# A three-layer decoder block on one core: chunk 0's second own terms and chunk 1's first state products moved ahead of the key units

## The reference, cut to what matters

```python
kh = jnp.einsum('bchd,bhde->bche', ki, S)
...
qh = jnp.einsum('bchd,bhde->bche', qi, S) - jnp.einsum('bhcs,bshe->bche', A, v_new)
o = qi + _ln(qh, w, b)
S = S - jnp.einsum('bchd,bche->bhde', ki * ei[..., None], v_new)
```

## Time and profile before

| | us |
|---|---|
| median of 3 runs | 380.12 |
| lowest and highest | 378.19 and 382.46 |
| the profiled execution, its time | 379.22 |
| its span in the trace | 377.5 |
| TensorE busy | 337.9 (89%) |
| VectorE busy | 264.6 (70%) |
| ScalarE busy | 202.0 (53%) |
| GpSimd busy | 75.7 (20%) |

### The profile page before, as it was taken

The page is one execution under the profiler, slowest core; times in us unless marked ns, Lnnn a source line. Parts: engine busy times, 40 slices in busy tenths (PEclk is TensorE's granted clock), DMA queues, the critical chain, the costliest instruction groups (busy, mean ns, idle before and its releaser), DMA issues.

```text
span 377.5 us, 11630 instructions
## 1 busy us (share of the span) xinstructions
PE 337.9 (89%) x5083; PEld 240.2 (64%) x5083; DVE 264.6 (70%) x537; ACT 202.0 (53%) x372; POOL 75.7 (20%) x91
## 2 busy tenths in 40 slices
PE   1999997996978785998999999999999999999974
PEld 1544585564534422687697796887977969866732
DVE  0499988897799899647263764855857739567795
ACT  1245974864545474346426555555565566576351
POOL 3009300000000000000062441522714405300100
PEclk9999999999999899799999999999999999999998
DMA  8997000000501203270040200200202000000000
GB/s 199 278 285 255 4 4 3 3 5 3 170 3 39 92 2 114 49 128 3 0 108 10 55 2 16 58 0 16 57 4 66 3 15 2 2 16 1 16 1 28
DMA packets 17987, 19.97 MB, mean 53 GB/s; under 512 B 3712, under 2 KB 15376, under 8 KB 17680
## 3 DMA queue, kind: packets, MB, share of 16 engines
q1 hardware_dynamic: 17328, 18.69, 18.3%
q10 hardware_dynamic: 608, 0.54, 0.7%
HBM read 18.04 MB, written 1.18 MB: 51 GB/s over the span
## 4 chain that ended last, share of the span: by engine, by line
PE 75%; DVE 13%; ACT 5%; issue 4%; DMA 1%; SPq 0%; POOLq 0%; POOL 0%; DVEq 0%; ACTq 0%
PE ps L795 14%; PE ps L729 14%; PE ps L550 6%; PE ps L772 5%; PE ps L787 5%; PE ps L665 4%; PE ps L503 3%; PE ps L814 3%; PE ps L841 2%; PE ps L745 2%; PE ps L531 2%; PE ps L521 2%; PE ps L620 2%; PE ps L763 2%; PE ps L655 2%
## 5 line engine op out<-in xcount | busy, mean ns | idle before, releaser
L729 PEld LDWEIGHTS ps<-x1t,xwq 128*128 128x128 f32 x512 | 59.2, 192 | 6.0 <-issue 4.2
L729 PE MATMUL ps<-x1t,xwq 128*128 128x128 f32 x512 | 62.1, 278 | 0.5 <-ACT x1t L1196 0.5
L795 PE MATMUL ps<-mvo,cxp 128*128 128x256 f32 x224 | 51.8, 383 | 0.5 <-ACT cxp L1207 0.5
L1909 POOL TENSOR_SCALAR rstd<-mv 128x1 f32<-128x1 f32 x20 | 4.4, 220 | 209.8 <-DVE mv L1650 209.8
L795 PEld LDWEIGHTS ps<-mvo,cxp 128*128 128x128 f32 x224 | 41.3, 190 | 6.6 <-ACT cxp L1207 0.8
L665 PE MATMUL ps<-ctxt,xwk 128*128 128x512 f32 x64 | 35.0, 656 | 3.9 <-ACT kt L1079 2.7
L1159 ACT ACTIVATE qt<-ps 128x512 f32<-128x512 f32 x32 | 19.1, 597 | 32.3 <-PE ps L729 32.3
L1077 ACT ACTIVATE ksq<-ps 128x512 f32<-128x512 f32 x32 | 19.0, 592 | 20.2 <-PE ps L665 13.3
L1079 ACT ACTIVATE kt<-ps,gks 128x512 f32<-128x512 f32 x32 | 21.9, 686 | 0.0
L1166 ACT ACTIVATE qsq<-ps 128x512 f32<-128x512 f32 x32 | 19.0, 593 | 4.7 <-PE ps L745 4.6
L772 PEld LDWEIGHTS ps<-kt,qt 128*64 128x64 f32 x512 | 16.2, 138 | 6.8 <-ACT qt L1159 3.8
(11 more groups left out here) (238 smaller groups left out, 681.3 us busy)
## 6 DMA issues: line engine op xcount, KB each, us to landing
rkb<-kscale SPq DMA_DIRECT2D x16, 256.0 KB, 4.1
ctx<-in_ctx_dram SPq DMA_DIRECT2D x4, 512.0 KB, 7.5
xwo<-in_L_xattn_Wo_dram SPq DMA_DIRECT2D x1, 2048.0 KB, 14.2
xwq<-in_L_xattn_Wq_dram SPq DMA_DIRECT2D x4, 512.0 KB, 4.4
w1n<-in_L_ffn_w_gate_up_dram SPq DMA_DIRECT2D x1, 1408.0 KB, 9.7
xwv<-in_L_xattn_Wv_dram SPq DMA_DIRECT2D x1, 1024.0 KB, 11.3
xwk<-in_L_xattn_Wk_dram SPq DMA_DIRECT2D x1, 1024.0 KB, 16.4
xn<-in_x_dram SPq DMA_DIRECT2D x2, 512.0 KB, 6.0
```

The source lines that it names most:

```text
L729: last = mm(bank(n % 2, P, t * P), xwq[qn][:, k * BANK + t * P:k * BANK + (t + 1) * P], x1t[:, (i % 2) * D + k * P:(i % 2) * D + (k + 1) * ...
L795: last = mm(bank(turn_banks[turn_of[("y", i, 0)]], D), context_of(i)[:, h * P:(h + 1) * P], mvo[:, h * D:(h + 1) * D], start=h == 0, stop= ...
```

## The change

PE: `own_terms(0,1)` and `state_products(1,0)` now stand directly behind the two `w2t` jobs, ahead of the wait for all jobs and of every key unit. `scores_ttt(1,1)` moves from behind `mvo` 7 to behind the first two key units. Ahead of `state_products(1,1)` there are 3 key units where there were 5; chunk 3 gets 13 where it had 11 (`KEY_PLACES`). `w2t` 0 takes bank 6, not 7.

ACT: the Sqrt with which the table is loaded moves from behind the first key unit to behind the copy of `s2`. All first three key units stand behind `state_root(1,0)` and the first output square; no key unit stands ahead of these.

DVE: `output_terms` is split. `query_terms(0)` and `query_terms(1)` (four products each) stand ahead of `after_own_terms(0,0)` and of `after_own_terms(0,1)`; the transpose stands behind `kb_rows(1)`. `a_masked(1)` moves behind `chain(1,0)`, `gate_terms` behind `after_own_terms(1,0)`.

```diff
--- before.py
+++ after.py
@@ -53,7 +53,7 @@
 GW = 2 * C + 32
 NKU = 2 * XH
 LT = NT - 1
-KEY_PLACES = [(1, 2), (2, 2, 1, 1, 2, 1), (2, 2, 1, 1, 2, 1), (2, 3, 3, 3)]
+KEY_PLACES = [(2, 1), (3, 2, 1, 1, 2, 1), (2, 2, 1, 1, 2, 1), (3, 3, 4, 3)]
 
 
 
@@ -313,7 +313,7 @@
             job("w2t", n, by="act")
         index_of = {(k, key): n for n, (k, key, _) in enumerate(jobs)}
         job_banks = [n % 8 for n in range(index_of[("s1", (0,))])]
-        job_banks += [(5, 6, 7, 0, 1, 2, 3)[n % 7] for n in range(len(jobs) - 1 - len(job_banks))] + [5]
+        job_banks += [(5, 6, 7, 0, 1, 2, 3)[n % 7] for n in range(len(jobs) - 2 - len(job_banks))] + [6, 5]
 
         def bank_left(n):
             return max(m for m in range(n) if job_banks[m] == job_banks[n])
@@ -621,7 +621,6 @@
                 done(last)
                 if n == 3:
                     scores_ttt(1, 0)
-            scores_ttt(1, 1)
             wait(emptied_by(index_of[("s1", (2,))]))
             pe.wait_ge(sem("diag_ready"), 2)
             bk = open_job("s2", 0)
@@ -639,6 +638,9 @@
                         last = nc.tensor.transpose(o[0:w, (t * KT + r) * P:(t * KT + r + 1) * P],
                                                    w2q[:, r * FF + k * P:r * FF + k * P + w], ident_b[:, :])
                 done(last)
+            wait(emptied_by(index_of[("s2", (0,))]))
+            own_terms(0, 1)
+            state_products(1, 0)
 
 
             def warm(bk, n):
@@ -678,12 +680,13 @@
                     key_unit(next(units))
 
             keys(KEY_PLACES[0][0])
-            own_terms(0, 1)
+            scores_ttt(1, 1)
             keys(KEY_PLACES[0][1])
             for c in range(1, NCH):
-                places = iter(KEY_PLACES[c])
-                state_products(c, 0)
-                keys(next(places))
+                places = iter(KEY_PLACES[c][1:])
+                if c > 1:
+                    state_products(c, 0)
+                    keys(KEY_PLACES[c][0])
                 state_products(c, 1)
                 keys(next(places))
                 if c < NCH - 1:
@@ -1056,6 +1059,7 @@
                 emptied(A(mvo[:, n * BANK:(n + 1) * BANK], bank(bk), ACT.Copy))
             bk = job_at("s2", 0)
             emptied(A(s2[:, :], bank(bk, D), ACT.Copy))
+            A(eps_t[:, 2:3], eps_t[:, 1:2], ACT.Sqrt)
             bk = job_at("w2t", 0)
             emptied(A(w2t[:, 0:3 * D], bank(bk).bitcast(BF16)[:, 0:3 * D], ACT.Copy))
             bk = job_at("w2t", 1)
@@ -1114,9 +1118,6 @@
                 for _ in range(n):
                     key_unit(next(units))
 
-            keys(KEY_PLACES[0][0])
-            A(eps_t[:, 2:3], eps_t[:, 1:2], ACT.Sqrt)
-            keys(KEY_PLACES[0][1])
             for c in range(1, NCH):
                 places = KEY_PLACES[c]
                 state_root(c, 0)
@@ -1506,12 +1507,13 @@
                 for h in range(2):
                     u_blocks(0, h)
 
+            def query_terms(hh):
+                dve.wait_ge(sem("prep_act"), emptied_by(index_of[("gate", (1, 1))])[1])
+                for c in range(NCH):
+                    V.scalar_tensor_tensor(out=chunk_half(sgR, c, hh), in0=kq_half(1, c, hh), scalar=wb[:, KT + hh:KT + hh + 1],
+                                           in1=chunk_half(tmp1, c, hh), op0=ALU.add, op1=ALU.mult).then_inc(sem("q_terms"), 1)
+
             def output_terms():
-                dve.wait_ge(sem("prep_act"), emptied_by(index_of[("gate", (1, 1))])[1])
-                for hh in range(KT):
-                    for c in range(NCH):
-                        V.scalar_tensor_tensor(out=chunk_half(sgR, c, hh), in0=kq_half(1, c, hh), scalar=wb[:, KT + hh:KT + hh + 1],
-                                               in1=chunk_half(tmp1, c, hh), op0=ALU.add, op1=ALU.mult).then_inc(sem("q_terms"), 1)
                 dve.wait_ge(sem("q_terms"), KT * NCH)
                 V.transpose(qbR[:, :], sgR[:, :]).then_inc(sem("out_terms"), 1)
 
@@ -1567,14 +1569,13 @@
             first_chains()
             for c in range(1, NCH):
                 p_rows(c)
+            query_terms(0)
+            after_own_terms(0, 0)
+            query_terms(1)
+            after_own_terms(0, 1)
+            kb_rows(1)
             output_terms()
-            after_own_terms(0, 0)
-            gate_terms()
-            after_own_terms(0, 1)
             for c in range(1, NCH):
-                if c == 1:
-                    kb_rows(c)
-                    a_masked(c)
                 if c == NCH - 1:
                     key_scales(0)
                 state_read(c, 0)
@@ -1584,12 +1585,16 @@
                     output_inverse(2 * c - 2)
                     out_c(c - 2)
                 chain(c, 0)
+                if c == 1:
+                    a_masked(c)
                 state_read(c, 1)
                 output_sums(2 * c - 1)
                 output_inverse(2 * c - 1)
                 chain(c, 1)
                 out_normed()
                 after_own_terms(c, 0)
+                if c == 1:
+                    gate_terms()
                 out_gated(c - 1)
                 after_own_terms(c, 1)
                 if c < NCH - 1:
```

## The result

The changed kernel's median is 380.33 us (12 runs), that of the kernel before 379.75 us (12 runs); the ratio of the recorded comparison is 1.006 with a 95% interval of 1.0031 to 1.0089. That is less than the 1% of the prediction's bound, so it counts as no change. The forecast was 380.7 and +1.0 us; the middle of the interval is +2.3 us. In a second comparison (experiment 5) the same kernel stood at 1.0012 (0.9982 to 1.0041), +0.5 us. The medians themselves lie 0.6 us apart in both comparisons (380.33 and 379.75, 379.60 and 378.95). So the two ratios put the loss at 0.6 and 0.1%, and whether there is one at all isn't settled. The ratios leave out executions that took over 1.5% more than the fastest of their kernel. The profiled execution took 381.24 us with a span of 379.5; the old one took 379.22 with 377.5.

A forecast was written before the change was run, and what follows sets the result against it. The prediction took this part of the chunk loop to be bound by arriving blocks of TensorE instructions. Gain and loss, −1.2 + 2.2 = +1.0 us, on 379.7 gave 380.7 us, range 377.0 to 383.2.

The forecast's parts named there:

- TensorE's opening: Start of the chunk loop on TensorE: own_terms(0,1) resumes at 62.6 us; state_products(1,0) ends at 67.8 instead of 71.6.
- VectorE's opening: VectorE up to chunk 1's state read: it comes at 68.4 us against 72.22, 3.8 us early.
- ScalarE: Moved table load and first key units on ScalarE: nothing on the path, up to 1 us if ScalarE is late.
- TensorE through chunk 1: Nine instruction blocks on TensorE take back most of the early start: gain of 1.2 us at chunk 2's state read.
- Chunk 2 and the key roots: Key units 16 and 17 come later, so VectorE waits 2.8 us for kinv: loss of 2.2 us at chunk 3's state read.
- Chunk 3: More key units ahead of state_products(3,1) and own_terms(3,1) fall into TensorE's idle time: nothing in the sum.
- rival 3: ScalarE's root in chunk 3 comes behind a late key unit: 2.2 us slower, 382.9 us; chance 0.12.
- The sum: Whole kernel: −1.2 + 2.2 = +1.0 us, a median of 380.7 us; chance 0.58.
- Rival 1: Instruction blocks do not bind in chunk 1: gain of 5.8 us at chunk 2's state read, 373.9 us; chance 0.05.
- rival 4: Opening groups stand still for blocks until their old times, and the key roots come in time: 379.7 us; chance 0.10.
- Rival 2: The gain of 1.2 us stays and the key roots come in time, loss 0: 378.5 us; chance 0.15.

The follow-up runs named there:

- experiment 5: The changed kernel itself, unaltered, run again for a second comparison and a second profile: 379.6 us, ratio 1.0012 to the kernel before.
- experiments 3: The changed kernel with 128 unused small matmuls of constants added on TensorE ahead of key unit 7 in chunk 1: 389.23 us, ratio 1.0266 to the kernel before.
- experiment 6: The changed kernel with 64 unused small matmuls of constants added on TensorE ahead of key unit 7: 384.74 us, ratio 1.0134 to the kernel before.
- experiment 4: The changed kernel with one long f32 matmul (128x128 by 512) added ahead of key unit 7: 381.53 us, ratio 1.0089 to the kernel before.
- experiment 1: The changed kernel with key_scales(0) moved from ahead of chunk 3's state read into VectorE's wait for ScalarE's root: 376.93 us, ratio 0.9936 to the kernel before.

## Why the prediction was right, step by step

The mechanism is as forecast in both profiles of the changed kernel: an early state read of chunk 1, stops at every 127 or 128 matmuls that take most of it back, and a wait for kinv that takes the rest. That the total came so near is partly luck, as the step on chunk 2 shows.

*TensorE's opening.* Predicted: own_terms(0,1) resumes at 62.6 with the 29th matmul, state_products(1,0) at 66.3 and ends at 67.8. Measured: a resumption at 61.79 behind 27 matmuls of the group, one at 65.65, an end at 67.7. The preparation ended 0.5 us earlier in this execution, the rest is the block count.

*VectorE's opening.* Predicted 68.4, measured 67.78. (The transposes of 2.24 us in the sum are 2.31 in the rows; nothing hangs on it.)

*ScalarE.* "Up to 1 us if ScalarE is late" was too little: VectorE waited 2.41 us for its root at 80.40, since TensorE's first two units ran at half clock and unit 4 came late. It cost nothing on the path, as TensorE released VectorE at the next state read in any case (1.98 us of wait at 96.73).

*TensorE through chunk 1.* Predicted: nine blocks at 3.7 to 3.97 us, resumption at 96.8, gain 1.2. Measured: 34.5 us for nine, 3.83 each, resumption at 96.28, gain 1.4. In the seven other executions that have this order up to there and nothing added, the state read of chunk 2 came between 94.5 and 96.5; in the two others with the old order it came at 95.4 and 98.8. The mean is 95.4 over eight against 97.5 over three. So a gain of about 2 us is likely, but one of the three old executions lies among the new ones, and single profiles scatter by 2 to 3 us. The forecast's 1.2 is right in sign; how near it is, one profile can't say: the second profile's 94.78 is 3.4 us early and below the 95.8 to 98.2 that the prediction named. That the blocks set this pace is shown by experiments 3 and 6, at 3.5 to 3.7 us for about 1.9 us of work; experiment 4 adds that long matmuls aren't free beside them. The Trainium skill's Runtime: NRT & Kernel Launch, Instruction fetch mechanics, has the next page fetched while the current one is run. The packets of experiment 4 agree with that; that a boundary's cost is mostly hidden does not hold for 32×32 matmuls, which use up a block in 1.3 to 2.1 us.

*Chunk 2 and the key roots.* This step decided the sign. U is the second L1440 of chunk 2, 107.31 in the first profile and 105.37 in the second.

| | predicted | first profile | second profile |
|---|---|---|---|
| own_terms(2,0) resumes | U + 3.77 | U + 2.47 | U + 4.10 |
| next resumption | U + 7.23 | U + 5.93 | U + 7.55 |
| unit 17 done on TensorE | U + 10.6 | U + 9.4 | U + 11.0 |
| krow ends | U + 12.4 | U + 11.3 | U + 12.9 |
| from krow's end until VectorE has kinv | 4.45 | 5.5 | 5.3 |
| VectorE has kinv | U + 16.8 | U + 16.85 | U + 18.2 |
| wait of VectorE | 2.8 | 3.21 | 3.72 |
| state read of chunk 3 | U + 17.4 | U + 17.31 | U + 18.7 |
| loss against U + 15.19 of before | 2.2 | 2.1 | 3.5 |

In the first profile two terms inside are off by 1.2 and 1.1 us and cancel. The stop in own_terms(2,0) was over 1.3 us sooner: the boundary stood 12 matmuls later than in the old order (98 ahead of it, not 86), and I read the difference as a block asked for before TensorE waited for the update, which no run tested. kinv took 2.9 us to land where it had taken 1.8. Before, SyncE issued the next 1 MB, for xwq, 1.9 us behind the reload; now it issues it 0.4 us behind. Over all fourteen profiles kinv landed in 2.6 to 3.7 us in the nine where xwq was issued 0.4 us behind, and in 1.6 to 1.8 us in the five where it was 1.1 us or more. I had carried the 4.45 us over from the old order without asking what stands behind the reload. So the loss of 2.1 us (2.2 predicted) is right as a sum, and partly by luck.

The second profile shows how much luck. Gain and loss were both larger, 3.4 and 3.5 us, and the sum is again near nothing. Counting from U hides the reason: U came 1.94 us earlier, but krow ended at 118.31, only 0.3 us earlier than the first profile's 118.63. TensorE began own_terms(2,0) at 107.83, 2.5 us behind U and no earlier than the 107.63 of the first profile. The root comes at TensorE's pace of blocks and not at VectorE's, so what VectorE gains at U it waits longer for kinv. That the wait is the cause experiment 1 shows: without it the changed kernel is faster than the old one, and the sum inside its own profile gives 3.2 us.

*Chunk 3.* Costed at nothing. The first profile had 1.23 us before ScalarE's root, 0.84 more than before: rival 3, at well under its price of 2.2. The second profile had 0.39. It goes with the clock behind TensorE's wait for the square of unit 19: experiment 4, with the low clock in this part, had 1.05 us, and experiment 6, with the full clock, 0.39.

*The sum.* On the first profile: +0.7 at the state read of chunk 3, +0.8 for the root, +0.5 for the later low clock: +2.0, the difference of the spans. On the second: +0.1 at the state read of chunk 3 and +0.1 at the end, a span of 377.5 as before. The forecast of +1.0 lies between the two ratios (+2.3 and +0.5 us) and above what the medians say (+0.6). Rival 1 (373.9) and rival 4 fell with the first profile: the stops stayed, the early landmark moved. Rival 2 (378.5, a ratio of 0.997) is what experiment 1 made: 0.9936, whose interval just holds it.

Experiment 1 gained 0.8 to 1.2% over the changed kernel by the ratios, 3.0 to 4.6 us. Its state read of chunk 3 is only 1.1 and 1.7 us earlier than in the two profiles of the changed kernel, but its krow ended 1.5 to 1.8 us later than theirs; counted inside the one profile the move saved 3.2 us, which agrees with the lower ratio. What stays open: where TensorE's stops fall in chunk 2 in one execution and another, and so the size of either term. Between executions the clock's low stretches and the blocks move by 2 us; one profile for each kernel does not average that.

## What to carry to other kernels

Moving work forward is paid where the displaced work ends up. Here the count of key units that had to be done before a distant, slow path (a root, a store, a reload) was the price, and it stood two chunks behind the edit. Before work is pushed back, look for everything that hangs on its last item, and place the consumer of a long round trip in a wait that exists anyway. If the slow path runs at the pace of another engine, count its times from that engine's landmarks and not from those of the engine that waits. And where one engine runs hundreds of tiny instructions, count blocks of 256 and not microseconds of work, and count them in the trace: an f32 matmul of this program is four instructions there, two matmuls and two weight loads.

## What the runs showed of the hardware that was not expected

- A block of 256 TensorE instructions costs 3.5 to 3.7 us when the stream is dense (experiments 3 and 6). The packet of the next block starts 1.0 to 1.2 us behind most resumptions, 2.4 us with long matmuls at the block's head (once), and 2.7 to 3.6 us where the DMA engines carry up to 390 GB/s of data (three times).
- Every f32 matmul of the program, large or 32×32, shows in the trace as two matmul instructions and two weight loads; a bf16 one shows as one matmul. I had counted the chunk loop's as one, and so added two blocks where I meant one.
- TensorE's granted clock fell to the lower level behind waits of 1.6 to 3 us, mostly for 3.4 or 6.8 us at a time, in different places in different executions of one kernel (0.66 of full clock over 66 to 71 us in the first profile, 1.00 in the old kernel's trace of that stretch). Not behind each such wait: experiment 4 had the same 2.18 us ahead of state_products(1,0) and 1.00 over 66 to 71 us. At the loop's end the low clock cost 1.9 us for eight f32 matmul instructions, and 14 throw-away matmuls in the waits took that back in the profiles.
- kinv (32 KB) landed in 1.6 to 1.8 us with nothing issued close behind it and in 2.6 to 3.7 us with 1 MB issued 0.4 us behind (five and nine profiles).
